# First attention of a decoder layer: the products of a batch dealt anew among the score groups

## The reference, cut to what matters

```
x = layernorm(x + self_attention(x))      # 16 heads of 32, 4 key/value heads, causal mask
x = layernorm(x + cross_attention(x, ctx))
x = layernorm(x + experts(x))

def self_attention(x):                    # b, t = 8, 256
    q = (x @ Wq).reshape(b, t, 4, 4, 32)  # key/value head, head in its group
    k = (x @ Wk).reshape(b, t, 4, 32)
    v = (x @ Wv).reshape(b, t, 4, 32)
    w = softmax(where(causal, q k^T / sqrt(32), -inf))
    return (w v).reshape(b, t, 512) @ Wo
```

## Time and profile before

| | |
|---|---|
| runs | 1929.87, 1932.19, 1934.29 us, median 1932.19 |
| the profiled execution | 1931.72 us; span of its instructions 1929.7 us |
| TensorE busy | 1775.5 us, 92% of the span |
| VectorE, ScalarE, GpSimd busy | 1253.9, 709.6, 270.4 us |
| first attention | up to about 337 us of the span |
| mean granted clock of TensorE | 0.959 of full speed |
| first scores of batch 0 and of batch 1 | at 27.81 and 59.70 us |
| first scores of batch 6 and of batch 7 | at 237.00 and 271.26 us |

### The profile page before, as it was taken

One profiled execution on the slowest core, in us unless ns is written; L12 is line 12 of the kernel. 1 busy time (PEld: TensorE's weight loads), 2 busy tenths in 40 slices (PEclk: granted clock), 3 DMA queues, 4 the chain that ended last, 5 costly groups with the idle time before them and its releaser, 6 DMA issues.

```text
span 1929.7 us, 37013 instructions
## 1 busy us (share of the span) xinstructions
PE 1775.5 (92%) x14528; PEld 1453.0 (75%) x14528; DVE 1253.9 (65%) x1943; ACT 709.6 (37%) x1492; POOL 270.4 (14%) x237
## 2 busy tenths in 40 slices
PE   4888786899995998999999999999999999999997
PEld 4777675688884776777887877878878878778886
DVE  4657764667775446566676675675766766756776
ACT  4545542212121425252343343433423433434331
POOL 1444533434331000000000000000000000000000
PEclk8879987899997999999999999999999999999999
DMA  4111120100001103021011020020120110300011
GB/s 150 51 37 46 60 69 12 61 13 22 11 0 42 53 1 89 14 54 55 14 40 59 7 92 6 8 90 6 43 55 13 44 54 6 91 6 9 11 49 44
DMA packets 51084, 76.67 MB, mean 40 GB/s; under 512 B 9153, under 2 KB 27713, under 8 KB 50241
## 3 DMA queue, kind: packets, MB, share of 16 engines
q1 hardware_dynamic: 51008, 75.62, 12.7%
HBM read 68.78 MB, written 6.82 MB: 39 GB/s over the span
## 4 chain that ended last, share of the span: by engine, by line
PE 59%; DVE 4%; issue 2%; ACT 1%; DMA 0%; SPq 0%; DVEq 0%; POOLq 0%; POOL 0%
PE pair L1847 9%; PE pair L1849 9%; PE pair L1848 9%; PE y_ps L1847 3%; PE y_ps L1848 3%; PE y_ps L1849 3%; PE qa_ps L1847 3%; PE qa_ps L1849 2%; PE qa_ps L1848 2%; PE pair L1984 2%; PE pair L1975 1%; PE pair L1974 1%; PE pair L1983 1%; PE qd_ps L2051 1%; PE qd_ps L2052 1%
## 5 line engine op out<-in xcount | busy, mean ns | idle before, releaser
L1847 PE MATMUL pair<-XH,GUH 128*128 128x512 f32 x800 | 313.3, 392 | 0.0
L1849 PE MATMUL pair<-XH,GUL 128*128 128x512 f32 x800 | 312.2, 390 | 0.0
L1848 PE MATMUL pair<-XL,GUH 128*128 128x512 f32 x800 | 312.2, 390 | 0.0
L1847 PEld LDWEIGHTS pair<-XH,GUH 128*128 128x128 f32 x800 | 150.5, 188 | 32.3
L1849 PEld LDWEIGHTS pair<-XH,GUL 128*128 128x128 f32 x800 | 150.3, 188 | 32.0
L1848 PEld LDWEIGHTS pair<-XL,GUH 128*128 128x128 f32 x800 | 150.6, 188 | 31.6
L1411 POOL TENSOR_TENSOR qb_raw<-qb_raw,qb_scale 128x704 f32<-128x704 f32 x8 | 16.5, 2059 | 1033.0 <-DMA qb_scale<-in_gu_scale 1033.0
L1421 ACT ACTIVATE HH<-h 128x512 fp32r<-128x512 f32 (+1 forms) x120 | 75.8, 632 | 183.5 <-DVE h L1754 96.5
L372 ACT ACTIVATE p<-scores_ps,nm 128x128 f32<-128x128 f32 (+1 forms) x256 | 103.8, 432 | 103.4 <-DVE nm L457 103.4
L1565 DVE TENSOR_TENSOR HL<-h,HH 128x512 fp32r<-128x512 f32 (+1 forms) x120 | 83.0, 691 | 83.8 <-ACT HH L1421 83.8
L1847 PE MATMUL y_ps<-DWH,HH 128*128 128x512 f32 (+1 forms) x288 | 118.1, 410 | 12.6 <-DVE xtok L1794 10.7
(11 more groups left out here) (337 smaller groups left out, 4205.2 us busy)
## 6 DMA issues: line engine op xcount, KB each, us to landing
gu_raw<-in_gu SPq DMA_DIRECT2D x20, 512.0 KB, 3.8
wrep<-soft_f SPq DMA_DIRECT2D x64, 128.0 KB
dw_raw<-in_dw SPq DMA_DIRECT2D x10, 512.0 KB, 3.9
xT_raw<-in_xT SPq DMA_DIRECT2D x8, 512.0 KB, 4.1
x_raw<-in_x SPq DMA_DIRECT2D x8, 512.0 KB, 3.6
VR<-v_rows SPq DMA_DIRECT2D x32, 128.0 KB, 2.5
out<-xtok SPq DMA_DIRECT2D x4, 1024.0 KB, 4.2
gu_raw<-in_gu SPq DMA_DIRECT2D x10, 384.0 KB, 3.3
```

Source lines behind the costliest of these rows:

```text
L1847: mm(out, wh, xh, start=first, stop=False)
L1848: mm(out, wh, xl, start=False, stop=False)
L1849: return mm(out, wl, xh, start=False, stop=last)
```

## The change

The steps of the first attention stay, but they are dealt to other places in every engine's list. On TensorE a middle batch becomes

```diff
-        def late(b, i, last):
-
-            return s_ps[:, i, :] if last else y_ps[:, i, :]
-
-        def turned(b, i, last):
-
-            return (s_ps[:, 2 + i, :] if last else y_ps[:, i, :]).rearrange("p (c t) -> p c t", c=KC)
+
+        QB, KB = y_ps[:, 0, :], y_ps[:, 1, 0:S]
+
+        def have(b, n):
+            return not isinstance(b, int) or b >= n
+
+        def late(b, i):
+
+            return s_ps[:, i, :] if isinstance(b, int) and b == B - 1 else y_ps[:, 2 + i, :]
+
+        def turned(b, i):
+
+            if isinstance(b, int) and b >= B - 2:
+                bank = s_ps[:, 2 + i, :] if b == B - 1 else y_ps[:, 2 * i, :]
+            else:
+                bank = y_ps[:, 2 + i, :]
+            return bank.rearrange("p (c t) -> p c t", c=KC)
+
+        def values_ps(b):
+            return s_ps if isinstance(b, int) and b == B - 1 else y_ps
+
+        def two_blocks(t, h):
+
+            return t[:, :, 2 * h:2 * h + 2, :].rearrange("p x a j -> p a x j")
+
+        def two_banks(b, h):
+            return values_ps(b)[:, 2 * h:2 * h + 2, 0:S].rearrange("p a (x j) -> p a x j", j=32)
 
...
-                sp.wait_ge(proj_done, NPJ * (n - 1) + 2)
+                sp.wait_ge(proj_done, NPJ * (n - 1) + 3)
...
             def batch(b, nxt):
+                tokens(b + 1, nxt)
+                values_out(b)
+                if have(b, 2):
+                    residual_in(b - 1)
+                if isinstance(b, int) and b == 0:
+                    sp.dma_start(way.k_raw[:], A["xwk"]).then_inc(way.l_k, 16)
+                    sp.dma_start(way.v_raw[:], A["xwv"]).then_inc(way.l_v, 16)
+                    for g in range(4):
+                        sp.dma_start(way.qk_bias[32 * g:32 * g + 32, :, :], A["xbqk"]).then_inc(way.l_b, 16)
+                if isinstance(b, int) and b == B - 1:
+                    sp.wait_ge(proj_done, NPJ * B)
+                    sp.dma_start(way.q_raw[:], A["xwq"]).then_inc(way.l_q, 16)
                 values_in(b)
...
+
+            for b in range(2):
+                batch(b, A["xT"][:, :, (b + 1) * S:(b + 2) * S])
+            with sp.Fori(2, B - 1) as b:
+                batch(b, A["xT"][:, :, bass.ds((b + 1) * S, S)])
+            batch(B - 1, A["cT"][:, :, 0:S])
+            residual_in(B - 1)
 
...
             def batch(b, first, last):
+                if have(b, 1):
+                    divide(b - 1, 3, 1)
+                if have(b, 2):
+                    deviation(b - 2, 1)
                 divide(b, 0, 0)
+                if have(b, 2):
+                    row_out(b - 2, 1)
                 divide(b, 0, 1)
                 divide(b, 1, 0)
                 divide(b, 1, 1)
...
+                divide(b, 2, 0)
+                divide(b, 2, 1)
+                if have(b, 1):
                     deviation(b - 1, 0)
...
+                divide(b, 3, 0)
+                if have(b, 1):
+                    row_out(b - 1, 0)
+                if last:
+                    divide(b, 3, 1)
                     deviation(b - 1, 1)
...
                     row_out(b - 1, 1)
...
                     deviation(b, 0)
                     deviation(b, 1)
                     row_out(b, 0)
                     row_out(b, 1)
...
+            over_batches(pool, batch, 3)
 
...
-            def o_high(b, i, last):
+            def o_high(b, h):
                 act.wait_ge(o_done, b + 1)
                 after(act, wo_done, 2 * b)
-                copy(OH[:, :, i * P:(i + 1) * P].rearrange("p g (a j) -> p a g j", a=4),
-                     (s_ps if last else y_ps)[:, :, i * P:(i + 1) * P].rearrange("p a (g j) -> p a g j", g=G)).then_inc(oh_rdy, 1)
-
...
             def batch(b, first, last):
+                values_copy(b)
                 exps(b, 0, 0)
                 exps(b, 0, 1)
...
+                queries_high(b, 1)
+                if have(b, 2):
+                    features_out(b - 2, 0)
+                    features_out(b - 2, 1)
                 split_x(b + 1)
+                exps(b, 1, 0)
+                exps(b, 1, 1)
+                if have(b, 1):
+                    o_high(b - 1, 0)
+                    o_high(b - 1, 1)
                 if first:
                     weights_high(way.l_k, way.WKH, way.k_raw)
...
+                exps(b, 2, 0)
+                exps(b, 2, 1)
                 if first:
                     weights_high(way.l_v, way.WVH, way.v_raw)
...
                 if not last:
                     queries_high(b + 1, 0)
...
+                    keys_high(b + 1)
                 exps(b, 3, 0)
...
                 exps(b, 3, 1)
...
                 if last:
...
+                    features_out(b - 1, 0)
+                    features_out(b - 1, 1)
+                    o_high(b, 0)
+                    o_high(b, 1)
                     weights_high(way.l_q, WQH, way.q_raw)
...
+                    features_out(b, 0)
+                    features_out(b, 1)
+            over_batches(act, batch, 3)
 
...
-                if g == 0 and unit == 0:
-                    after(dve, o_done, b)
+                if g == 0:
+                    after(dve, (half_done, o_done)[unit], b)
...
+            def o_low(b, h):
+                dve.wait_ge(oh_rdy, 2 * b + h + 1)
+                sub(two_blocks(OL, h), two_banks(b, h), two_blocks(OH, h).bitcast(F32)).then_inc(ol_rdy, 1)
+
...
             def batch(b, first, last):
...
+                second = isinstance(b, int) and b == 1
+                if have(b, 1):
+                    reciprocals(b - 1, 3, 1)
                 maxima(b, 0)
...
+                if have(b, 2):
+                    residual(b - 2, 1)
+                if second:
+                    weights_low(0, way.WKH, way.WKL, way.k_raw)
+                if have(b, 1):
+                    probs_turned(b - 1, 3, 0)
+                if have(b, 2):
+                    norm_out(b - 2, 1)
+                if have(b, 1):
                     probs_turned(b - 1, 3, 1)
                 reciprocals(b, 0, 0)
+                queries_low(b, 1)
+                maxima(b, 1)
+                reciprocals(b, 0, 1)
+                split_x(b + 1)
+                reciprocals(b, 1, 0)
                 probs_turned(b, 0, 0)
...
+                reciprocals(b, 1, 1)
+                if have(b, 1):
+                    o_low(b - 1, 0)
+                maxima(b, 2)
+                if have(b, 1):
+                    o_low(b - 1, 1)
                 probs_turned(b, 0, 1)
...
                 probs_turned(b, 1, 0)
...
+                reciprocals(b, 2, 0)
                 probs_turned(b, 1, 1)
...
                 reciprocals(b, 2, 1)
                 if not last:
                     queries_low(b + 1, 0)
                 maxima(b, 3)
...
+                if have(b, 1):
+                    residual(b - 1, 0)
+                probs_turned(b, 2, 0)
                 if not last:
                     keys_low(b + 1)
...
+                reciprocals(b, 3, 0)
+                if have(b, 1):
+                    norm_out(b - 1, 0)
+                probs_turned(b, 2, 1)
+                if second:
+                    weights_low(1, way.WVH, way.WVL, way.v_raw)
                 if last:
...
+                    reciprocals(b, 3, 1)
+                    probs_turned(b, 3, 0)
+                    residual(b - 1, 1)
+                    norm_out(b - 1, 1)
                     probs_turned(b, 3, 1)
...
+                    o_low(b, 0)
+                    o_low(b, 1)
+                    residual(b, 0)
+                    residual(b, 1)
                     norm_out(b, 0)
                     norm_out(b, 1)
                     weights_low(2, WQH, WQL, way.q_raw)
...
+            over_batches(dve, batch, 3)
 
...
+                if n == 1:
+                    pe.wait_ge(r_rdy, 2 * (B - 1))
...
             def queries(b, w):
                 if w == 0:
                     pe.wait_ge(xl_rdy, b + 1)
-                elif not isinstance(b, int) or b > 0:
-                    pe.wait_ge(v_rdy, b + 1)
+                    after(pe, ol_rdy, 2 * (b - 2) + 1)
...
-            def values(b, last):
-                pe.wait_ge(lo_rdy, NLO * (b + 2) if not last else NLO * B)
-                after(pe, xt_rdy, 2 * b)
+            def values(b):
+                if isinstance(b, int) and b == B - 1:
+                    pe.wait_ge(exp_done, 2 * G * B)
+                else:
+                    pe.wait_ge(lo_rdy, NLO * (b + 2))
+                    pe.wait_ge(v_rdy, b + 2)
+                    after(pe, xt_rdy, 2 * b)
                 pe.wait_ge(l_v, 64 * (b + 1))
                 pe.wait_ge(pb_rdy, 2 * G * (b + 1))
                 alone(pe, past)
                                 continue
                             for kv in range(KV):
                                 rows = slice(32 * a, 32 * a + 32)
-                                done = mm((s_ps if last else y_ps)[HD * kv:HD * kv + HD, a, i * P:(i + 1) * P],
```

(48 more changed lines are left out.)

175 lines of the change are left out of this document (27 added, 148 removed).

## The result

| kernel | median of runs, us | range | runs |
|---|---|---|---|
| before | 1931.03 | 1926.62 to 1934.29 | 4 |
| changed | 1912.51 | 1911.67 to 1913.05 | 4 |

The ratio is 0.9905, 95% interval 0.9884 to 0.9926: 18 us faster. I had forecast 1893 with 1880 to 1910, so 39 us; I got half of it, and the time lies above the range. The profiled execution took 1911.67 us, its span is 1909.6. Three views of it show where the rest went.

A forecast was written before the change was run, and what follows sets the result against it. No engine is full; the chain of scores, maxima and exponentials (28.1 us a batch) and TensorE's work (26.8) bound it. Head 3.5 + batches 1 to 6 25.8 + tail 9.6 = 39 less: 1893, range 1880 to 1910.

The forecast's parts named there:

- gap by gap: Gaps 0 to 3, each from one group's scores to the next's in a middle batch: 7.3, 7.0, 8.9, 7.0 us.
- The new wait of gap 2: ScalarE's exponentials of group 2 wait for group 0's second transpose, behind the maxima on VectorE: 1.9 us a batch.
- rival D: The wait in gap 2 is not there, the order of tiles misjudged: 1.9 x 7 less, 1880; chance 0.08.
- Head: Value rows and second queries go behind the first scores; waiting for the low keys costs 1.0: 3.5 us less.
- The values at 5.43 us in every batch: Gap 1, TensorE: value products run from 8.8 to 14.2 without their 3.24 us wait; step 7.0, before 8.32.
- The second weight split: VectorE, end of batch 1, moved there from batch 0: about 2.3 us, making the next maxima 2.0 late.
- The early clock: Half-clock stretches in the first batches: 2.0 us added to the six batches' 181.8.
- Tail: Last batch: 5.0 less up to its values, 4.6 less behind them (0 if the clock falls): 9.6 us less.
- rival B: VectorE's queue becomes the bound, held up by GpSimd's divides: 1.2 us a batch, 8 us, 1901; chance 0.13.
- Rival C: Clock falls to half in the values: values 1.5 longer, scores 1.2, 2.7 x 6 = 16 us, 1909; chance 0.14.
- Rival E: ScalarE stands at the next tokens' split ahead of group 1's exponentials: slower, 1941 at a 13 us landing; chance 0.03.

The follow-up runs named there:

- wait put back: Changed kernel with the middle batches' value products also waiting for the first exponentials of group 1, an idle of about 3.5 us: 1941.31 us (1.0053).
- turn-first version: Changed kernel with VectorE's second transpose of group 0 put ahead of the maxima of group 2: 1905.39 us (0.9859).

## Why the prediction was half right

**What bounds the kernel, gap by gap.** Right where the code is repeated. The steps of batch 4 are 7.55, 7.02, 8.86, 7.03, forecast 7.3, 7.0, 8.9, 7.0. The new wait of gap 2 is there; the timeline of ScalarE in batch 5 of the changed kernel has the first exponential of group 2 released by a turn:

```profile
211.17 0.37 ACT L390 ACTIVATE p<-scores_ps,nm 128x128 f32<-128x128 f32 x1 [4.56 <-DVE PB L486]
```

So rival D is out. The rest of the sum:

- **Head**: 3.5 forecast, 3.85 measured.
- **The values at 5.43 us in every batch: the step that failed.** I took their duration from one row, batch 6 of the kernel before, and it held three things that I did not part. The products themselves take 4.24 at the full clock. The half clock behind the 3.2 us idle made that 5.43; it was also the shortest of the seven instances, with batch 5's (in batches 1 to 7 of the kernel before: 6.9, 7.5, 6.4, 6.0, 5.4, 5.4, 7.0). And batch 6 was repeated code; in code that is run first the fetch makes it 7.3 to 9.6 us. The kernel before had that limit too, but it showed less: its values ran at a granted clock of 0.50 to 0.54 in the batches run first, a piece of 128 lasts some 3.17 us at that pace (the first of the earlier trace rows), nearly as long as the next one takes to come, and there was no hole in batches 1 and 7 and one of 0.29 us in batch 2. Without the wait the clock stays up, but the pieces still come 3.4 to 3.7 us apart, so the values were no shorter than before. Per batch, against 30.3: 4.6 in batch 1, 5.35 in batch 2, 4.05 in batch 3, 0.4 together in 4 to 6, less the 4.0 that I had added for the split and the early clock: 10.4, which is 25.8 less 15.4. By steps, against batch 4's 7.02 and 8.86: gap 1 of batches 1 to 3 is 1.8, 2.1 and 3.0 longer, gap 2 0.4, 1.0 and 1.2. The first two of gap 1 are at a clock of 1.00, so they are the holes alone; in gap 2 it is the clock (0.81 to 0.83).
- **The loop's start**, moved from 2 to 3 by the diff, I costed at nothing, without a word. The batch that changed its kind took 4.1 us less in one run that moved it (batch 3, 30.23 for 34.35) and 3.2 more in the other (batch 4, 33.63 for 30.46).
- **The second weight split**: right in size, for 2.0 forecast 2.3 us in gap 0 of batch 2 (9.59 for 7.31 in batch 3).
- **The early clock**: 2.0 forecast; gap 0 of batch 1 takes 9.83 for 7.55, 2.3 more, at a granted clock of 0.70 behind an idle of 3.74 us, with no hole in it: ScalarE's exponentials stand behind the copy of the value rows, and these came late at that clock.
- **Tail: 9.6 less forecast, 1.2 more measured.** Group 3's scores come at 28.65 instead of 23.2, for the values of batch 6 (9.62) and the half clock behind them. The values of batch 7 start at 43.4, forecast 36.5: another 1.4 us, of which 0.9 is rival B's hand-over, below. Behind their start to the second attention it is 26.97, where I had 23.0 (27.63 less 4.6): values and third context product take 12.3 where I had 8.3 (7.36 with two holes, and 4.9 at a granted clock of 0.53); behind them both kernels take 14.7. 6.9 and 4.0 make 10.9.

**Rival C** had the right place and nearly the right size (1909, measured 1912.5), but the wrong cause, so the size is luck: it let the clock fall in the values of all batches. In batches 4 to 6 of the profiled execution the clock is 1.00, and in 1 to 3 it falls behind the holes. That holes are needed for it is not so: when the changed kernel ran again, gap 3 of batch 4 took 8.37 us instead of 7.03 at a granted clock of 0.80, without a hole ahead of it. I had priced its worst case by the last batch of the kernel before, 12.9 us; that stretch already had holes of 0.45 and 0.47 us behind 128 and 256 records, in the trace of the kernel before, and I read all of it as clock.

**Rival B** shows in the last batch alone. In the timelines of VectorE and GpSimd of the changed kernel, in the last batch:

```profile
286.74 1.41 DVE L510 TENSOR_SCALAR xs<-xs,mv,rstd 128x512 f32<-128x512 f32 x1
```

```profile
286.83 1.04 POOL L316 TENSOR_TENSOR p<-p,rinv 128x512 f32<-128x512 f32 x1
```

The normalised rows take 1.41 us there and 0.51 to 0.55 in batches 1 to 6, while the divide keeps its 1.04: here VectorE was the one held up, though its row begins 0.09 us earlier. Which of them had asked first the rows do not show. (Another of 1.50 us at 316.35 was there in the kernel before too.) In the repeated batches VectorE kept its usual time, as forecast, and rival B cost nothing.

**Rival E** is out: no exponential waits for the token load.

The instruction fetch is in the Trainium skill, Runtime: NRT & Kernel Launch, section Instruction fetch mechanics: blocks of 256 instructions, brought by a DMA queue of their own ahead of their use, and mostly hidden. These runs agree on the block (pieces of 128 matmuls and as many loads) and on the queue; "mostly hidden" does not hold for the value products in code that runs first.

**What stays open.** A packet comes about 1.1 us behind the start of a piece and the next piece 2.3 to 2.7 us behind the packet; together these are the 3.4 to 3.7 us between pieces (up to 4.0 in other versions). What sets the two the runs do not show; one load moved out of the way took 1.3 us from one hole. Nor do they show why the clock falls behind some holes and short idles and not behind others.

## What to carry to other kernels

Read a duration from more than one instance, and ask of each whether its code had run before: the loop's later passes give a price that batches written out, the loop's first pass and what stands behind it do not have. Before you count on a faster clock, ask what else limits the stretch: here the instructions came no faster than TensorE had used them at the half clock. Where many short products stand together, look at the pieces of the timeline for holes at equal counts. Letting the loop begin early takes the holes out of a batch, though here the total did not show it by itself.

## What the runs showed of the hardware that was not expected

- Pieces of 128 matmuls with 128 weight loads start 3.4 to 3.7 us apart in code that runs first (138.97 and 142.71 in batch 3; 175.02 and 178.48 with the loop one later; up to 4.0 in other versions), while TensorE uses up such a piece in 1.9 us at the full clock (288 records in 4.24) and in some 3.1 at the half clock (116.33, wait put back). Behind the first piece the hole is 1.0 to 1.3 us in the changed kernel, 2.54 beside a large load.
- An idle of TensorE of 3.5 us ahead of such products brought no instruction packet on q8 (batches 2 and 3 with the wait put back; batches 1 and 2 of the kernel before); the first packet came 1 to 2 us behind the start of the products.
- Later passes of a loop whose body has some 509 matmuls and as many weight loads on TensorE bring no instruction packet at all (0 in batches 4 to 6); a batch that runs first brings 4 or 5, which at 256 instructions each is about its 1018.
- 1.13 us of idle behind 4.22 us of value products was enough for the granted clock to be 0.69 in the next 4 us (the second window of the turn-first version), while 1.09 us in batch 4 of the changed kernel left it at 1.00 (174.21 to 178.21).
